# Feed-forward down products: VectorE adds a place's four PSUM banks to x in one instruction instead of two banks twice

## The reference

```python
x = x + _L0_xattn_ref(_layernorm(x, axis=-1), ctx_2048, mask_BxS2_bk0)
x = x + _L0_attn_ref(_layernorm(x, axis=-1), L0_attn_Wq, L0_attn_Wk, L0_attn_Wv, L0_attn_Wo)
x = x + _L0_ffn_ref(_layernorm(x, axis=-1), L0_ffn_w_gate, L0_ffn_w_up, L0_ffn_w_down)
...
gate = jnp.einsum('bsd,hd->bsh', x, w_gate)      # 1024 -> 4096
up = jnp.einsum('bsd,hd->bsh', x, w_up)
gated = jax.nn.silu(gate) * up
return jnp.einsum('bsh,dh->bsd', gated, w_down)  # 4096 -> 1024
```

## Time and profile before

| what | value |
|---|---|
| median of 3 runs | 1507.94 us (1506.26 to 1508.06) |
| the profiled execution: its own time | 1506.29 us |
| the profiled execution: its span | 1504.5 us |
| PE busy (matmuls) | 1477.5 us, 98% of the span |
| VectorE, ScalarE, GpSimd busy | 766.9, 555.1, 869.7 us |
| granted TensorE clock, mean | 0.997 of full speed |

### The profile page before, as it was taken

One profiled execution on the slowest core, in us unless ns is written; L12 is line 12 of the kernel. 1 busy time (PEld: TensorE's weight loads), 2 busy tenths in 40 slices (PEclk: granted clock), 3 DMA queues, 4 the chain that ended last, 5 costly groups with the idle time before them and its releaser, 6 DMA issues.

```text
span 1504.5 us, 23233 instructions
## 1 busy us (share of the span) xinstructions
PE 1477.5 (98%) x7988; PEld 1203.7 (80%) x7988; DVE 766.9 (51%) x1232; ACT 555.1 (37%) x1099; POOL 869.7 (58%) x712
## 2 busy tenths in 40 slices
PE   7999999999999999999999999999999999999998
PEld 5766887887878888888888888888888888888886
DVE  5776054162261496935626626526536436436446
ACT  4557132132231254334344343343433343433442
POOL 1233211302212121389789788788798798798795
PEclk9999999999999999999999999999999999999999
DMA  9992200101201000021111111111121121121123
GB/s 380 400 367 97 83 29 28 56 28 38 74 0 56 29 1 22 20 65 56 49 63 56 49 63 49 56 63 49 51 67 49 42 77 38 53 70 35 56 63 112
DMA packets 42950, 114.18 MB, mean 76 GB/s; under 512 B 4896, under 2 KB 5152, under 8 KB 40480
## 3 DMA queue, kind: packets, MB, share of 16 engines
q1 hardware_dynamic: 42480, 113.27, 22.1%
q10 hardware_dynamic: 432, 0.39, 0.1%
HBM read 109.45 MB, written 4.19 MB: 76 GB/s over the span
## 4 chain that ended last, share of the span: by engine, by line
PE 95%; DVE 2%; DMA 1%; issue 1%; SPq 1%; ACT 0%; DVEq 0%
PE ps L1281 38%; PE ps L1301 18%; PE ps L940 10%; PE ps L941 9%; PE ps L942 9%; PE ps L974 3%; PE ps L1014 2%; PE ps L992 2%; PE ps L1082 1%; DMA ctx<-in_ctx 1%; PE ps L946 1%; PE ps L1125 1%; DVE x L1702 1%; SPq L344 0%; DVE x L1478 0%
## 5 line engine op out<-in xcount | busy, mean ns | idle before, releaser
L557 POOL TENSOR_TENSOR b_lo<-blk,b_hi 128x512 fp32r<-128x512 f32 x180 | 231.8, 1295 | 49.8 <-ACT b_hi L835 41.2
L1702 DVE TENSOR_TENSOR x<-ps,x 128x1024 f32<-128x1024 f32 x210 | 242.2, 1211 | 0.0
L470 POOL TENSOR_TENSOR w_lo<-raw,w_hi 128x2048 fp32r<-128x2048 f32 x16 | 73.3, 4584 | 287.5 <-ACT w_hi L677 287.5
L1281 PE MATMUL ps<-xT_hi,b_hi 128*128 128x512 f32 x480 | 186.7, 389 | 0.0
L1281 PE MATMUL ps<-xT_lo,b_hi 128*128 128x512 f32 x480 | 186.7, 389 | 0.0
L1281 PE MATMUL ps<-xT_hi,b_lo 128*128 128x512 f32 x480 | 186.7, 389 | 0.0
L1301 PE MATMUL ps<-b_hi,b_hi 128*128 128x512 f32 x420 | 166.5, 396 | 0.0
L1301 PE MATMUL ps<-b_lo,b_hi 128*128 128x512 f32 x420 | 163.8, 390 | 0.0
L1301 PE MATMUL ps<-b_hi,b_lo 128*128 128x512 f32 x420 | 163.6, 389 | 0.0
L1676 DVE TENSOR_TENSOR hid<-ps,kept 128x512 f32<-128x512 f32 x60 | 41.5, 692 | 233.7 <-PE ps L1281 193.8
L557 POOL TENSOR_TENSOR b_lo<-s_sum,b_hi 128x512 fp32r<-128x512 f32 x105 | 136.2, 1297 | 35.9 <-ACT b_hi L835 35.9
(11 more groups left out here) (155 smaller groups left out, 3227.6 us busy)
## 6 DMA issues: line engine op xcount, KB each, us to landing
blk<-in_blocks SPq DMA_DIRECT2D x180, 256.0 KB, 2.7
ctx<-in_ctx SPq DMA_DIRECT2D x64, 512.0 KB, 10.1
raw<-in_w SPq DMA_DIRECT2D x19, 1024.0 KB, 4.8
x<-in_x SPq DMA_DIRECT2D x8, 512.0 KB, 7.2
ext_row<-in_ext SPq DMA_DIRECT2D x8, 512.0 KB, 13.2
out<-x SPq DMA_DIRECT2D x16, 256.0 KB, 2.6
mask<-in_mask ACTq DMA_DIRECT2D x1, 224.9 KB, 6.0
extT<-in_ext_t ACTq DMA_DIRECT2D x1, 128.0 KB, 4.4
```

The costliest lines, as they stand in the source:

```text
L470: pool.tensor_tensor(w_lo[wslot][:, :], raw[slot][:, :], w_hi[wslot][:, :].bitcast(F32), ALU.subtract).then_inc(split_done[slot], 1)
L557: pool.tensor_tensor(b_lo[slot][:, :], src[:, :], b_hi[slot][:, :].bitcast(F32), ALU.subtract).then_inc(block_lo, 1)
L1281: mm = pe.matmul(ps[:, bank, :], stat[a], moving[b], start=first and m == 0, stop=(s == 3 and m == 2), skip_group_check=True)
L1702: dve.tensor_tensor(part, ps[:, bank:bank + 2, :], part, ALU.add).then_inc(down_added, 1)
```

## The change

VectorE's `add` takes a whole place at once: it waits for both halves of the place, adds four banks in one instruction of 128 x 4 x 512, and increments `down_added` by 2 at its end. The seven pairs of adds of a chunk become seven adds. The order around place 0 differs too: before, half 0 of place 0 was added ahead of `low(c, 2)` and half 1 behind it; now all of place 0 is added between `low(c, 2)` and `low(c, 3)`.

```diff
-        def part_of_x(place, q):
+        def part_of_x(place):
             half, col = ADD_TO[place]
-            return x[:, half * 4 + 2 * q:half * 4 + 2 * q + 2, col * HALF:(col + 1) * HALF]
+            return x[:, half * 4:half * 4 + 4, col * HALF:(col + 1) * HALF]
...
-            def add(c, place, q):
-                dve.wait_ge(pair_done, (c - 1) * ADDS + (2 * place + q + 1))
+            def add(c, place):
+                dve.wait_ge(pair_done, (c - 1) * ADDS + 2 * (place + 1))
                 dve.wait_ge(down_added, added(c - 1, 6, 1))
                 if place in ADDED_TWICE:
-                    dve.wait_ge(down_added, added(c, ADDED_TWICE[place], q))
-                bank = DOWN_BANKS[place] + 2 * q
-                part = part_of_x(place, q)
-                dve.tensor_tensor(part, ps[:, bank:bank + 2, :], part, ALU.add).then_inc(down_added, 1)
+                    dve.wait_ge(down_added, added(c, ADDED_TWICE[place], 1))
+                bank, part = DOWN_BANKS[place], part_of_x(place)
+                dve.tensor_tensor(part, ps[:, bank:bank + 4, :], part, ALU.add).then_inc(down_added, 2)
...
-                add(c, 0, 0)
                 low(c, 2)
-                add(c, 0, 1)
+                add(c, 0)
                 low(c, 3)
-                add(c, 1, 0)
-                add(c, 1, 1)
-                for place in range(2, 7):
-                    for q in range(2):
-                        add(c, place, q)
+                for place in range(1, 7):
+                    add(c, place)
```

## The result

The changed kernel takes 1557.56 us (median of 4 runs, 1554.38 to 1559.10) against 1507.10 us before (4 runs, 1506.18 to 1508.06). The ratio is 1.033, interval 1.0316 to 1.0348: 3.3% slower. The forecast of 1532 had the direction, but the time lies outside its range of 1527 to 1545. The profiled execution took 1556.10 us with a span of 1554.3, 49.8 us more than before's span. Its mean granted clock is 0.984, where it was 0.997.

The account below looks back on a forecast made before the run. TensorE, busy 95% of the span, was taken as the bound. Fourteen chunks at + 1.58 us (22.1) plus 2.9 for the last chunk and tail give 25.0 us more: 1531.3 to 1532.9, forecast 1532, range 1527 to 1545.

Parts of the forecast that it names:

- the clock was priced as a rival: Behind place 2's new pause the clock halves, 1.4 us a fall; 1553 if in all 15 chunks; chance 0.08.
- the release at place 2: Place 2 opens only after place 0's big add, 1.96 us late, costing 1.85 us a chunk.
- a `low` slowed by GpSimd: Upper end of the forecast's own range, 1538: GpSimd slows a low by 0.17 to 0.2 us, twice a chunk.
- the later places: Places 4, 5, 6 and the next chunk's gate: late by 0.04 us, cost 0, with 0.07 us to spare.
- +1.58 forecast: Sum of a chunk: + 1.85 at place 2, + 0.08 at place 3, - 0.35 for the old loss.
- a sign of being wrong: The prediction would be wrong if TensorE is late at more than two places of a chunk.
- VectorE's answer to a finished place: From a place's end to VectorE's add that waited for it: 0.04 us, taken from ScalarE's row.
- rival 2: Places after place 3 wait too, through VectorE's slower answer or a 2.42 us add: 1541 to 1545; chance 0.12.
- 0.08, at place 3: Place 3 opens 0.19 us late behind place 1's big add, costing 0.08 us a chunk.
- the 0.35 us that a chunk lost before: Loss of a chunk's down products before the change, 19.39 us against 19.04 at pace; taken off the sum.
- the later stores: Last chunk and tail: stores begin later as place 4 is added in one go; together 2.9 us.
- Rival 1: VectorE limits the down products, so merging removes both old waits at places 2 and 3: 1502.5; chance 0.03.

Follow-up runs that it names:

- e1: The changed kernel with 8 extra matmuls a chunk, results unused, ahead of place 1's own: 1539.45 us, 1.0216 to before.
- e9: The changed kernel with 2 extra matmuls a chunk, results unused, ahead of place 1's own: 1540.68 us, 1.0223 to before.
- e2: The kernel before with low(c, 2) ahead of both half-adds of place 0, nothing else changed: 1520.58 us, 1.0086.
- e5: The kernel before with places 1 to 6 added four banks at a time, place 0 left as two half-adds: 1527.28 us, 1.0135.
- e6: The changed kernel with 8 extra matmuls a chunk, and GpSimd's first hidden sum started only after low(c, 2): 1539.97 us, 1.0218 to before.
- e10: The kernel before with place 0 alone added four banks at a time, between low(c, 2) and low(c, 3): 1551.71 us, 1.0298.
- e3: The kernel before with adds of four banks for places 2 to 6 only: 1520.13 us, 1.0082.
- e8: The kernel before with adds of four banks for places 4, 5 and 6 only: 1510.77 us, 1.0022.
- e7: The kernel before, half-adds kept, with low(c, 3) made by GpSimd in place of VectorE: 1502.55 us against 1507.42, 0.997.

## Why the prediction was wrong

**Right: the bound and the mechanism.** TensorE names half 0 and gets its banks only when all four are added. The wait stands at place 2, the small ones at place 3 and later; VectorE's saved time is worth nothing; TensorE has no new wait for GpSimd. The big add lasts 2.288 us in the mean (2.28 forecast). The span ends 4.6 us after the last add (1549.7 to 1554.3), as forecast. The direction was no luck: it follows from this mechanism.

**The step that failed: the clock was priced as a rival with a chance of 0.08.** Its price was right: 1.4 us a fall forecast, 1.5 measured. What failed is the argument against it. I set the new pause of 1.96 us between pauses of 2.8 us, of which one had a fall behind it and one had none, and a single stretch of 1.9 us with hardly a matmul in it and no fall. One quiet stretch of that size is no evidence about 15. And the third of the pauses of 2.8 us, which the prediction counts but leaves out of this argument, has a fall in the trace of before as well:

```profile
451.05:454.46 3.41, 3.41 (x10) 2.65 (x9) 0.95 (x4) 0.00 (x0) 0.00 (x0) 0.50 0.80 279
```

So it was two of three there. In the twelve profiles of this case, 30 of the 36 such pauses in attention have a fall behind them. The new pause came out at 11 falls in 15 chunks, 11 x 1.5 = 16.5 us. e1 and e9 show that this part is the clock's: extra work takes 17 to 18 us away, the granted clock is 1.00, and place 2 still opens as late as the add of place 0 makes it. Without the falls the time is about 1540 us (e1 and e9), inside the forecast's range; they alone carried it out. The Trainium skill, "TensorE: Matmul & The Clock Gate", HAM oscillation, describes matmul bursts that run slow behind each wait; its example has waits of 3 to 5 us. Here the trace agrees for 11 of 15 pauses of 1.9 us, and not for pauses of 1.5 us or less in e9, e2 and e5.

**A term that was mis-sized: the release at place 2.** Forecast late by 1.96 us, measured 2.29. The 0.33 between is `low(c, 2)`: I took its 0.68 us from the old timeline, where it ran beside GpSimd's sum for 0.1 us only. Moved 0.35 us earlier, it ran beside it for 0.46 and took 1.00. The forecast's range had a `low` slowed by GpSimd, but by 0.17 to 0.2 us, twice a chunk. e6 shows the cause: with GpSimd's sum out of the way `low(c, 2)` took 0.69.

**A term that was put too low: the later places.** A chunk at full clock costs +2.10 for +1.58 forecast, so behind the 0.33 some 0.2 us is left. Places 3 and 6 open late there, so TensorE is late at three places of a chunk, which the prediction had named as a sign of being wrong. VectorE's answer to a finished place was taken as 0.04 us. Place 3's last matmul ends at 1295.82 + 0.39 = 1296.21 and the add begins at 1296.30, 0.09 later; at place 4, which has one more wait on VectorE, it is 1298.93 to 1299.13, 0.20. That is rival 2's mechanism in a small size. e10, in which places 1 to 6 are half-adds again, gives its price. Only place 2 is late there (15 waits), and it has 10 falls between its first and last add of place 0, like the changed kernel, but these 14 chunks take 846.88 us (680.22 to 1527.10) and not 849.42: 0.18 us a chunk less. Of that the forecast had 0.08, at place 3. Some 0.1 us a chunk stays open; half of it may be that the sum took off all of the 0.35 us that a chunk lost before, though its two old waits (0.08 and 0.22) explain only 0.30.

**The sum, made again from the trace:** from the first big add to the last of place 0 are 14 chunks, 679.96 to 1529.38: 849.4 us against 14 x 57.47 = 804.6. The 44.8 are 14 x 2.10 = 29.4 of release and 15.4 of clock, in 10 falls. The last chunk's release and fall add about 3.6. What is left of 49.8, about 1.4, I put down to the later stores; it was not measured apart.

Rival 1 is refuted as it stood: merging alone gained nothing in any run (e3, e5, e8). What is true in it, e7 shows: place 3's old wait did hang on VectorE's queue, and went when an instruction ahead of place 1's adds was moved to another engine.

Open: which pauses let the clock fall. The chunks with and without a fall look alike on all engines ahead of the pause. The changed kernel's four runs spread over 4.7 us where before's spread over 1.9, which would fit one to three falls more or less, but that was argued, not shown. Part of any such spread lies outside the chunks: e1's profile has two falls in attention and e9's three, with the same code there, and e9 comes to its chunks 1.4 us later; so a difference of that size between two of these runs says nothing of an edit.

## What to carry to other kernels

An instruction that is merged also merges its release: ask of each merged half who waited for it, and how far behind its queue the engine is at that place. Where an engine runs a backlog, the earliest increment is worth more than the fixed cost of an instruction; where it has none, merging is harmless and worthless. And where pauses of TensorE in the trace have falls behind them, a new pause of nearly their size is to be priced with the clock's fall as a likely case, not a remote one; look behind every such pause before giving the chance.

## What the runs showed of the hardware that I had not expected

- Behind a pause of 1.9 us between dense matmuls the granted clock fell to half for about 3.4 us in 11 of 15 chunks. With 0.45 us of the pause filled it fell in none. Extra matmuls that compute nothing of use made the kernel 17 to 18 us faster.
- A VectorE subtraction on SBUF alone of 512 elements takes 0.67 to 0.69 us, and 0.85 to 1.07 us when a GpSimd operation overlaps it; the adds that read PSUM kept 2.27 to 2.29 us beside GpSimd's work.
